# Queries one group further ahead, numerators at the front of the iteration, new orders of work

## The chip, the cores and the metric

The kernel runs on one core of a Trainium2 chip. The metric is the device time of the kernel in microseconds, as the median of several runs. The profile is of one further execution, and its times are counted from the start of its span.

## What is computed

```
xn  = (x - mean(x)) / sqrt(var(x) + 1e-5)              # x: 8 x 2048 x 256, float32
q, k, v = split(xn @ Wqkv + bqkv)                      # 256 each
qp, kp  = elu(q) + 1, elu(k) + 1
kv  = sum over s of kp[s] v[s]^T;  k_sum = sum over s of kp[s]     # per batch
attn = (qp @ kv) / (qp @ k_sum + 1e-6)
z   = layer_norm(xn + attn) * g1 + b1
h   = silu(z @ Wg + bg) * (z @ Wu + bu)                # 682 hidden columns
s   = layer_norm(z + h @ Wd + bd) * g2 + b2
g   = silu(xn @ ternary(weight)^T * scale)
out = x + s * g
```

## The kernel before

The 16384 rows are 32 groups of 512, four groups a batch; a group is four tiles of 128 rows. Float32 products are made as three products of rounded parts: every left and right operand has a high part (`_high`, written by ScalarE as fp32r) and a low part (`_low`, the rest, subtracted by VectorE). K and XK (the keys and the sum of k x^T over a batch) run five groups ahead of the feed-forward part, since kv of a batch must be known before its first numerator.

One iteration `i` works on several groups at once: the keys on group a = i + 5, its x on a + 1, the attention on q = i + 1, the feed-forward part on f = i, and the last layer norm on i - 1. The fill (i = -1) does what must be there before, iteration 31 is the end and 32 the drain. What each engine does in an iteration, and in which order, is written out by hand: a list of steps for TensorE (`TENSOR_JOBS`), ScalarE, VectorE and GpSimd, one set for the steady iterations, one for the fill, one for the end. Each engine takes its list in order and waits by semaphores; `run_steps` skips a step whose group does not exist or that the fill has done. SyncE issues all DMAs from a loop of its own.

TensorE's jobs of an iteration: K (2 jobs, 12 products of 256 columns each), Q (2 x 6 of 512), KV (2, every fourth iteration), B (2 x 8 of 256, the gate g), N (4 x 6 of 258, the numerator and denominator of a tile of 128 rows), G and U (5 each, 6 of 512), GU (one more, the last 42 hidden columns), D (five of 12 products of 256 and D 5 with 4; D 4 and D 5 come in the next iteration), XK (4 x 6 of 256). All but D and XK write to a ring of five banks: a job waits until what the fifth job before it wrote has been read. A bank of Q is freed by `q_elu`, of K by `k_add`, of N by `attn` (semaphore r), of G by `silu_gate`, of U by `h_low`, of B by `silu_tern`, of GU by `h_rows`.

The steps that the prediction names: `q_exp` (ScalarE: relu and exp of a half of q), `q_elu` (VectorE: the max with it), `q_high`, `q_low` (the parts); `k_add`, `k_exp`, `k_max`, `k_high`, `k_low` the same for the keys, `sum_k` (GpSimd) adds up kp; `x_res` (ScalarE) writes the normed x to rz, `attn` (VectorE) adds numerator times reciprocal to it and takes its statistics, `q_aggregate`, `q_rstd`, `attn_norm`, `z_rows` norm it, `z_turn` transposes it by blocks, SyncE sends it to DRAM in four pieces and reads it back, `zT_high` and `zT_low` make its parts, on which G 0 waits; `silu_gate`, `h_rows`, `h_high`, `h_low` make the hidden rows, `tail_again` (GpSimd) copies the last 32 of them twice for D 5; `ffn_rows`, `last_stats`, `last_rows`, `last_gain`, `last_offset`, `last_gate`, `last_add` finish the group before; `a_stats`, `a_norm`, `x_turn`, `x_high`, `x_low`, `xn_high`, `xn_low` prepare the next x. q, its exp and its parts have one buffer each (`qp`, `qp_h`, `qp_l`): `q_exp` of a group waits for the `q_low` of the one before, and `q_high` waits for all its N jobs. ScalarE needs another table for exp than for silu.

## Time and profile before

| | |
|---|---|
| median of three runs | 1260.41 us (1255.08 to 1262.71) |
| the profiled execution | 1252.69 us, of it the span 1251.0 us |
| TensorE busy | 1212.3 us (97%), 7499 products |
| VectorE, ScalarE, GpSimd busy | 1067.6 (85%), 957.5 (77%), 795.8 us (64%) |
| ScalarE table loads | 118, 1283 ns each |
| DMA | 116.64 MB, 93 GB/s |
| clock granted to TensorE | 0.993 of full speed |

Products overlap in the profile (each is shown some 0.17 us longer than it holds up the next), so their starts tell more than their lengths. Instructions that follow each other without a wait overlap by up to 0.1 us on the other engines too. The line of every ScalarE instruction is that of its helper (L680), and of every product L1201. A bracket behind a row gives the idle time before it and what ended it.

### The profile page before, as it was taken

Reading aid. Unit: us, or ns where it says so; the run is one execution under the profiler, and the core shown is the slowest. Engines: PE = TensorE matmul, PEld = TensorE weight load, DVE = VectorE, ACT = ScalarE, POOL = GpSimd, SP = SyncE. Lnnn points to the kernel's source line nnn. Section 1 sums busy time; section 2 is a strip of 40 time slices with the busy share of each in tenths; the row PEclk is TensorE's granted clock in tenths of the full one; section 3 lists DMA queues with packets and bytes.
Section 4 is the critical chain, followed back from the end, with each engine's and each line's share of the span. In section 5 each row is a group of like instructions: output and inputs, shape, how many; then the busy total and the mean of one; then the engine's idle time right before and its main releaser. Section 6 shows DMA issues by size and latency. Waiting matters only on the chain.

```text
span 1251.0 us, 23909 instructions
## 1 busy us (share of the span) xinstructions
PE 1212.3 (97%) x7499; PEld 1078.8 (86%) x7499; DVE 1067.6 (85%) x2473; ACT 957.5 (77%) x1540; POOL 795.8 (64%) x994
## 2 busy tenths in 40 slices
...
GB/s 193 66 71 85 82 88 75 112 119 119 99 71 85 102 119 119 100 75 81 101 118 118 117 71 93 76 119 119 118 86 81 83 107 102 68 68 68 68 52 34
DMA packets 138594, 116.64 MB, mean 93 GB/s; under 512 B 12387, under 2 KB 122853, under 8 KB 138470
## 3 DMA queue, kind: packets, MB, share of 16 engines
...
q8 instruction: 61, 1.00, 0.3%
...
## 4 chain that ended last, share of the span: by engine, by line
DVE 43%; PE 31%; ACT 11%; issue 11%; DMA 2%; SPq 1%; POOL 1%; DVEq 0%; ACTq 0%; POOLq 0%
PE bank L1201 21%; DVE st L887 7%; PE d_bank L1201 6%; DVE bank L1038 5%; DVE rz L997 4%; PE xk_bank L1201 3%; DVE ht L1052 3%; ACT rz L680 3%; DVE xa L928 3%; DVE xn L917 2%; DVE h_l L1048 2%; ACT hs L680 2%; ACT h_h L680 2%; DVE qp L979 2%; DVE kp L957 2%
## 5 line engine op out<-in xcount | busy, mean ns | idle before, releaser
L1201 PE MATMUL bank<-zT_h,wgu_h 128*128 128x512 f32 x704 | 279.2, 397 | 5.8 <-DVE zT_l L1028 5.8
L1201 PE MATMUL bank<-zT_l,wgu_h 128*128 128x512 f32 x704 | 279.4, 397 | 0.0
L1201 PE MATMUL bank<-zT_h,wgu_l 128*128 128x512 f32 x704 | 279.2, 397 | 0.0
L596 POOL TENSOR_TENSOR ksum<-ksum,kp 128x256 f32<-128x256 f32 x120 | 90.5, 754 | 183.8 <-DVE kp L964 182.6
L680 ACT ACTIVATE h_h<-bank 128x512 fp32r<-128x512 f32 x160 | 95.1, 595 | 133.5 <-DVE bank L1038 133.5
L1201 PE MATMUL d_bank<-wd_l,h_h 128*128 128x256 f32 x640 | 180.6, 282 | 0.0
L1201 PE MATMUL d_bank<-wd_h,h_h 128*128 128x256 f32 x640 | 180.3, 282 | 0.1
L1201 PE MATMUL d_bank<-wd_h,h_l 128*128 128x256 f32 x640 | 180.4, 282 | 0.0
L1201 PEld LDWEIGHTS bank<-zT_l,wgu_h 128*128 128x128 f32 x704 | 132.7, 189 | 31.8
L1201 PEld LDWEIGHTS bank<-zT_h,wgu_h 128*128 128x128 f32 x704 | 132.7, 189 | 30.4 <-issue 6.5
L1201 PEld LDWEIGHTS bank<-zT_h,wgu_l 128*128 128x128 f32 x704 | 133.2, 189 | 24.4
L680 ACT ACT_TABLE_LOAD x118 | 151.4, 1283 | 3.4 <-PEq L1396 0.8
L680 ACT ACTIVATE hs<-bank,hb 128x512 f32<-128x512 f32 x192 | 131.0, 682 | 28.4 <-PE bank L1201 27.7
L1048 DVE TENSOR_TENSOR h_l<-bank,h_h 128x512 fp32r<-128x512 f32 x160 | 109.7, 686 | 28.3 <-ACT h_h L680 24.9
L573 POOL TENSOR_TENSOR rstd<-ve,neg_half 128x4 f32<-128x4 f32 x64 | 66.4, 1038 | 104.9 <-DVE ve L898 104.9
L1038 DVE SCALAR_TENSOR_TENSOR bank<-bank,hb,hs 128x512 f32<-128x512 f32 x160 | 118.8, 742 | 9.8 <-PE bank L1201 7.7
L1201 PEld LDWEIGHTS d_bank<-wd_h,h_h 128*128 128x128 f32 x640 | 120.3, 188 | 3.6 <-DVE h_l L1048 0.3
L1201 PEld LDWEIGHTS d_bank<-wd_h,h_l 128*128 128x128 f32 x640 | 120.6, 188 | 3.0
L1201 PEld LDWEIGHTS d_bank<-wd_l,h_h 128*128 128x128 f32 x640 | 120.7, 189 | 0.0
L606 POOL TENSOR_TENSOR rz<-rz,g2b 128x256 f32<-128x256 f32 x124 | 92.3, 744 | 39.7 <-ACT rz L680 39.7
L887 DVE BATCH_NORM_STATS2 st<-rz 128x6 f32<-128x256 f32 x256 | 99.5, 420 | 4.4
L680 ACT ACTIVATE rz<-rz,nmr,rstd 128x256 f32<-128x256 f32 x128 | 71.9, 591 | 41.0 <-DVE nmr L1007 41.0
...
## 6 DMA issues: line engine op xcount, KB each, us to landing
...
```

What stands on the lines that cost most here:

```text
L573: eng.tensor_tensor(dst, ve[:, k, :], neg_half[:, 0:1].to_broadcast([P, TILES]), ALU.pow).then_inc(S[f"rs{k}"], 1)
L596: eng.tensor_tensor(ksum[:, slot, :], ksum[:, slot, :], part, ALU.add).then_inc(S["ks"], 1)
L606: eng.tensor_tensor(row_, row_, g2b[:, :], ALU.mult).then_inc(S["a"], 1)
L680: return eng.activation(out_, in_, func, **kw).then_inc(S[name], 1)
L887: eng.bn_stats(st[:, k, t, :], rows).then_inc(S[f"bn{k}"], 1)
L917: eng.tensor_scalar(normed(g)[:, t, :], xa[:, g % 2, t, :], mv[:, 0, t, 0:1], rstd0[:, g % LN0, t:t + 1], ALU.subtract, ALU.mult).then_inc ...
L928: eng.transpose(whole.rearrange("p (j t n) -> p t j n", t=TILES, n=BLOCK), xn[:, :, :].rearrange("p t (j n) -> p t j n", n=BLOCK)).then_in ...
L997: eng.scalar_tensor_tensor(out=rz[:, g % RZ, t, :], in0=num[:, 0:D], scalar=den[:, n % 2, 1:2], in1=rz[:, g % RZ, t, :], op0=ALU.mult, op1 ...
L1038: eng.scalar_tensor_tensor(out=hidden(g, c)[0:rows, :], in0=up, scalar=hb[0:rows, HC + c:HC + c + 1], in1=hs[0:rows, n % 2, :], op0=ALU.ad ...
L1048: eng.tensor_tensor(h_l[:, slot, :], hidden(g, c)[:, :], h_h[:, slot, :].bitcast(f32), ALU.subtract).then_inc(S["hl"], 1)
L1052: eng.scalar_tensor_tensor(out=part, in0=part.bitcast(f32), scalar=less_h[UT:UT + TH, 0:1], in1=hidden(g, c)[0:TH, :], op0=ALU.mult, op1=A ...
L1201: ins = eng.matmul(dst, left, right, start=first and n == 0, stop=last and n == len(pairs) - 1, **kw)
```

## The change

Q, `q_exp`, `q_elu`, `q_high` and `q_low` work on group q + 1 = i + 2 instead of q. The fill makes them for group 1 too. In the steady list of TensorE the N jobs now stand ahead of G 0, behind K 1; the Q jobs stand between U 2 and B 1. The other lists are ordered anew: on VectorE `attn` comes ahead of `h_rows 0`, `k_low` ahead of `z_turn`, `q_elu` and `q_low` in the second half; on ScalarE `zT_high` comes first, `x_res 0` and `x_res 1` ahead of `silu_gate 0` and `x_res 2`, `x_res 3` behind it, `q_exp` and `q_high` in the second half; on GpSimd `tail_again 0` and `1` follow each other and `sum_k 3` and `z_g1 3` come last. In the fill one of the three warm jobs comes earlier, `setup_gu_high_0` and `_1` come later on ScalarE, and `setup_gu_low_1` comes just ahead of `kv_bias` on VectorE. The lists of the end change a little. SyncE's program is unchanged. The diff without the lists of the end and of the fill on three engines:

```diff
--- before.py
+++ after.py
@@ -86,74 +86,75 @@
 
 LATE_D = 4
 TENSOR_JOBS = steps("""
-    Q 0, K 0, D 4, Q 1, KV 0, KV 1, D 5, K 1, G 0, U 0, G 1, U 1, G 2, B 0, N 0, N 1, U 2, N 2, B 1,
-    N 3, G 3, D 0, D 1, U 3, G 4, XK 0, U 4, XK 1, XK 2, XK 3, GU 5, D 2, D 3, TZ 0, TZ 1""")
+    K 0, D 4, KV 0, KV 1, D 5, K 1, N 0, N 1, N 2, N 3, G 0, U 0, G 1, U 1, G 2, B 0, U 2, Q 0, Q 1,
+    B 1, G 3, D 0, D 1, U 3, G 4, XK 0, U 4, XK 1, XK 2, XK 3, GU 5, D 2, D 3, TZ 0, TZ 1""")
 SCALAR_STEPS = steps("""
-    xk_copy 0, q_exp 0, zT_high 0, zT_high 1, q_high 0, q_exp 1, kv_high 0, k_exp 0, kv_high 1, x_res 0,
-    silu_gate 0, q_high 1, x_res 1, silu_gate 1, last_rows 0, h_high 0, h_high 1, x_res 2, last_rows 1,
-    silu_gate 2, last_rows 2, x_res 3, silu_tern 0, h_high 2, silu_tern 1, silu_gate 3, k_exp 1,
-    k_high 0, z_rows 0, last_rows 3, z_rows 1, k_high 1, z_rows 2, z_rows 3, silu_gate 4, h_high 3,
-    xn_high 0, h_high 4, silu_gate 5, x_high 0, x_high 1, h_high 5, xn_high 1""")
+    zT_high 0, zT_high 1, xk_copy 0, x_res 0, kv_high 0, kv_high 1, k_exp 0, x_res 1, silu_gate 0,
+    last_rows 0, x_res 2, last_rows 1, x_res 3, last_rows 2, silu_gate 1, h_high 0, h_high 1,
+    silu_gate 2, silu_tern 0, k_exp 1, last_rows 3, h_high 2, q_exp 0, q_exp 1, z_rows 0, k_high 0,
+    z_rows 1, z_rows 2, z_rows 3, silu_gate 3, k_high 1, silu_tern 1, q_high 0, x_high 0, silu_gate 4,
+    q_high 1, x_high 1, h_high 3, xn_high 0, xn_high 1, silu_gate 5, h_high 4, h_high 5""")
 VECTOR_STEPS = steps("""
-    k_add 0, q_elu 0, zT_low 0, zT_low 1, q_low 0, kv_bias 0, kv_bias 1, ffn_rows 0, q_elu 1,
-    ffn_rows 1, k_max 0, kv_low 0, last_stats 0, kv_low 1, k_add 1, h_rows 0, last_shift 0, q_low 1,
-    h_rows 1, h_low 0, h_low 1, a_stats 0, attn 0, attn 1, h_rows 2, attn 2, h_low 2, attn 3, a_norm 0,
-    q_aggregate 0, x_turn 0, attn_norm 0, k_low 0, k_max 1, k_low 1, z_turn 0, h_rows 3, h_low 3,
-    h_rows 4, h_rows 5, x_low 0, x_low 1, h_low 4, h_low 5""")
+    zT_low 0, k_add 0, zT_low 1, kv_bias 0, kv_bias 1, kv_low 0, kv_low 1, ffn_rows 0, ffn_rows 1,
+    k_add 1, last_stats 0, attn 0, last_shift 0, attn 1, attn 2, attn 3, h_rows 0, h_rows 1, h_low 0,
+    a_stats 0, h_low 1, k_max 0, h_rows 2, a_norm 0, q_aggregate 0, x_turn 0, attn_norm 0, k_max 1,
+    h_low 2, q_elu 0, q_elu 1, k_low 0, z_turn 0, h_rows 3, k_low 1, q_low 0, h_rows 4, q_low 1,
+    h_low 3, x_low 0, x_low 1, h_rows 5, h_low 4, h_low 5""")
 GPSIMD_STEPS = steps("""
-    sum_k 0, xn_low 0, last_rstd 0, last_gain 0, last_offset 0, sum_k 1, xn_low 1, last_gain 1, z_g1 0,
-    last_offset 1, last_gain 2, a_rstd 0, last_gate 0, last_gate 1, last_offset 2, q_rstd 0, sum_k 2,
-    last_gain 3, last_add 0, last_offset 3, last_gate 2, last_add 1, z_g1 1, z_g1 2, sum_k 3,
-    last_gate 3, tail_again 0, last_add 2, last_add 3, z_g1 3, tail_again 1""")
+    xn_low 0, last_rstd 0, last_gain 0, last_offset 0, last_gain 1, z_g1 0, last_offset 1, last_gate 0,
+    last_gain 2, xn_low 1, last_gate 1, a_rstd 0, q_rstd 0, last_add 0, last_add 1, last_offset 2,
+    last_gain 3, sum_k 0, sum_k 1, z_g1 1, last_offset 3, last_gate 2, z_g1 2, last_add 2, last_gate 3,
+    last_add 3, sum_k 2, tail_again 0, tail_again 1, sum_k 3, z_g1 3""")
 
...
 FILL_JOBS = fill("""
-    TX 0 0, TX 0 1, warm 9 1, K 0 0, TX 1 0, K 0 1, K 1 0, TX 1 1, XK 0 0, XK 0 1, setup_bias_0 0 0,
-    XK 0 2, XK 0 3, K 1 1, setup_bias_1 0 0, TX 2 0, TX 2 1, XK 1 0, XK 1 1, setup_bias_2 0 0, K 2 0,
-    XK 1 2, XK 1 3, K 2 1, TX 3 0, TX 3 1, Q 0 0, XK 2 0, K 3 0, XK 2 1, XK 2 2, XK 2 3, Q 0 1, TX 4 0,
-    K 3 1, TX 4 1, setup_sum 0 0, XK 3 0, XK 3 1, K 4 0, setup_transposes 0 0, XK 3 2, XK 3 3, KV 0 0,
-    KV 0 1, warm 9 2, K 4 1, B 0 0, B 0 1, N 0 0, XK 4 0, N 0 1, N 0 2, N 0 3, warm 9 0, XK 4 1, XK 4 2,
-    XK 4 3, TZ 0 0, TZ 0 1""")
+    TX 0 0, warm 9 2, TX 0 1, K 0 0, K 0 1, TX 1 0, warm 9 0, TX 1 1, K 1 0, setup_bias_0 0 0, XK 0 0,
+    XK 0 1, XK 0 2, XK 0 3, K 1 1, setup_bias_1 0 0, TX 2 0, TX 2 1, XK 1 0, XK 1 1, XK 1 2, K 2 0,
+    XK 1 3, K 2 1, TX 3 0, TX 3 1, Q 0 0, K 3 0, XK 2 0, setup_sum 0 0, XK 2 1, XK 2 2, XK 2 3,
+    setup_bias_2 0 0, K 3 1, TX 4 0, setup_transposes 0 0, Q 0 1, XK 3 0, XK 3 1, K 4 0, TX 4 1, XK 3 2,
+    XK 3 3, KV 0 0, K 4 1, KV 0 1, Q 1 0, Q 1 1, N 0 0, N 0 1, N 0 2, B 0 0, N 0 3, B 0 1, warm 9 1,
+    XK 4 0, XK 4 1, XK 4 2, XK 4 3, TZ 0 0, TZ 0 1""")
...
@@ -185,7 +186,7 @@
         return FILL_JOBS
     jobs = []
     for kind, n in order_of(i, FILL_JOBS, TENSOR_JOBS, END_JOBS):
-        g = {"K": a, "XK": a, "TX": a + 1, "G": f, "U": f, "GU": f, "D": f - 1 if n >= LATE_D else f}.get(kind, q)
+        g = {"K": a, "Q": q + 1, "XK": a, "TX": a + 1, "G": f, "U": f, "GU": f, "D": f - 1 if n >= LATE_D else f}.get(kind, q)
         if kind == "TZ" and ZT0 <= g < ZT1:
             continue
         if 0 <= g < GROUPS and (kind != "KV" or q % GPB == 0) and (kind, g, n) not in FILL_JOBS:
@@ -871,8 +872,8 @@
                     "setup_gu_high_0": (a, lambda: gu_high(0)), "setup_gu_high_1": (a, lambda: gu_high(1)),
                     "setup_d_high": (a, setup_d_high), "setup_row_0": (a, lambda: row_copy(0)),
                     "setup_row_1": (a, lambda: row_copy(1)), "setup_row_2": (a, lambda: row_copy(2)),
-                    "zT_high": (f, zT_high), "xk_copy": (q, xk_copy), "q_exp": (q, q_exp), "k_exp": (a, k_exp),
-                    "q_high": (q, q_high), "k_high": (a, k_high), "kv_high": (q, kv_high),
+                    "zT_high": (f, zT_high), "xk_copy": (q, xk_copy), "q_exp": (q + 1, q_exp), "k_exp": (a, k_exp),
+                    "q_high": (q + 1, q_high), "k_high": (a, k_high), "kv_high": (q, kv_high),
                     "silu_gate": (f, silu_gate), "x_res": (q, x_res), "h_high": (f, h_high),
                     "silu_tern": (q, silu_tern), "xT_high": (a + 1, xT_high), "x_high": (a + 1, x_high), "z_rows": (q, z_rows),
                     "xn_high": (a + 1, xn_high), "last_rows": (last, last_rows)})
@@ -1184,8 +1185,8 @@
                     "setup_d_bias": (a, setup_d_bias), "setup_q_low": (a, lambda: setup_qk_low(0)), "setup_bq": (a, setup_bq),
                     "setup_gu_low_0": (a, lambda: setup_gu_low(0)), "setup_gu_low_1": (a, lambda: setup_gu_low(1)),
                     "setup_ternary": (a, setup_ternary), "setup_ternary_parts": (a, setup_ternary_parts),
-                    "zT_low": (f, zT_low), "a_stats": (a + 1, a_stats), "q_elu": (q, q_elu), "k_add": (a, k_add),
-                    "q_low": (q, q_low), "k_max": (a, k_max), "k_low": (a, k_low), "kv_bias": (q, kv_bias),
+                    "zT_low": (f, zT_low), "a_stats": (a + 1, a_stats), "q_elu": (q + 1, q_elu), "k_add": (a, k_add),
+                    "q_low": (q + 1, q_low), "k_max": (a, k_max), "k_low": (a, k_low), "kv_bias": (q, kv_bias),
                     "kv_low": (q, kv_low), "ffn_rows": (last, ffn_rows),
                     "h_rows": (f, h_rows), "attn": (q, attn), "h_low": (f, h_low), "a_norm": (a + 1, a_norm), "x_turn": (a + 1, x_turn), "x_low": (a + 1, x_low),
                     "q_aggregate": (q, lambda g, _: aggregate(1, g)), "last_stats": (last, last_stats),
```

## Rows read from the trace of the kernel before

**Rows 1.** Windows of TensorE: stretch, its length, busy time (x products), clock granted, DMA share, GB/s.

```profile
60.00:86.00 26.00, 20.87 (x134) 0.93 0.35 99
86.00:1100.00 1014.00, 1011.55 (x6342) 1.00 0.33 96
1100.00:1225.00 125.00, 117.67 (x680) 0.99 0.22 64
```

**Rows 2.** Timeline of VectorE: start, length, operation; `h_low 5` of three iterations in a row.

```profile
636.39 2.35 DVE L1052 SCALAR_TENSOR_TENSOR ht<-ht,less_h,hs 62x512 fp32r<-62x512 f32 x1
...
674.82 2.36 DVE L1052 SCALAR_TENSOR_TENSOR ht<-ht,less_h,hs 62x512 fp32r<-62x512 f32 x1
...
711.60 2.36 DVE L1052 SCALAR_TENSOR_TENSOR ht<-ht,less_h,hs 62x512 fp32r<-62x512 f32 x1
```

**Rows 3.** Chain of waits, 624 to 642 us: start, length, engine and line.

```profile
626.02 0.99 PE xk_bank L1201 x6
627.00 1.40 PE bank L1201 x6
628.40 2.13 PE xk_bank L1201 x18
...
631.93 2.87 PE d_bank L1201 x24
```

**Rows 4.** Timeline of VectorE, 682 to 704 us: stats, next add, attn, both k_low.

```profile
682.74 1.40 DVE L887 BATCH_NORM_STATS2 st<-rz 128x6 f32<-128x256 f32 x4
...
684.88 0.68 DVE L957 TENSOR_TENSOR kp<-bank,bk1b 128x512 f32<-128x512 f32 x1
...
691.14 0.14 DVE L991 TENSOR_SCALAR den<-bank 128x1 f32<-128x1 f32 x1
...
692.38 0.14 DVE L991 TENSOR_SCALAR den<-bank 128x1 f32<-128x1 f32 x1
...
700.50 0.68 DVE L973 TENSOR_TENSOR kp_l<-kp,kp_h 128x512 fp32r<-128x512 f32 x1
...
702.75 1.08 DVE L973 TENSOR_TENSOR kp_l<-kp,kp_h 128x512 fp32r<-128x512 f32 x1 [0.97 <-ACT kp_h L680]
```

**Rows 5.** The tile xk_bank: what its engine sat idle for, us and times.

```profile
  DVE kp_l L973: 14.0, 28
```

**Rows 6.** Timeline of TensorE, the waits for z; in brackets the idle time before.

```profile
84.60 0.38 PE L1201 MATMUL bank<-wqk_h,xT_h 128*128 128x256 f32 x1 [1.26 <-DVE zT_l L1028]
...
1184.81 0.47 PE L1201 MATMUL bank<-zT_h,wgu_h 128*128 128x512 f32 x1 [1.51 <-DVE zT_l L1028]
...
1214.29 0.71 PE L1201 MATMUL d_bank<-wd_h,ht 128*128 128x256 f32 x4 [1.41 <-POOL ht L657]
1216.26 0.47 PE L1201 MATMUL bank<-zT_h,wgu_h 128*128 128x512 f32 x1 [1.25 <-DVE zT_l L1028]
```

**Rows 7.** Timeline of ScalarE: two table loads with their neighbours; rows of one iteration.

```profile
0.80 1.28 ACT L680 ACT_TABLE_LOAD   x1 [0.80 <-PEq L1396]
6.20 0.63 ACT L680 ACTIVATE wqk_h<-qp 128x512 fp32r<-128x512 f32 x1 [4.11 <-DMA qp<-in_L_attn_Wqkv_dram]
...
67.57 1.28 ACT L680 ACT_TABLE_LOAD   x1 [0.53 <-POOL wd_l L663]
...
614.41 0.60 ACT L680 ACTIVATE rz<-rz,norm 128x256 f32<-128x256 f32 x1
614.91 0.60 ACT L680 ACTIVATE rz<-xq,nmr,rstd 128x256 f32<-128x256 f32 x1
```

**Rows 8.** Timelines of VectorE and ScalarE: the last z_turn and the zT_high it feeds.

```profile
1204.50 1.25 DVE L1017 STREAM_TRANSPOSE xa<-rz 128x1024 f32<-128x1024 f32 x1 [2.64 <-ACT rz L680]
...
1213.61 1.15 ACT L680 ACTIVATE zT_h<-xa 128x512 fp32r<-128x512 f32 x2 [2.55 <-DMA xa<-z_turned]
```

**Rows 9.** Timeline of GpSimd around 636 us: last_add 2 and 3, z_g1 3.

```profile
636.08 1.42 POOL L625 TENSOR_TENSOR rz<-rz,xq 128x256 f32<-128x256 f32 x2
637.47 0.72 POOL L646 TENSOR_TENSOR rz<-rz,g1b 128x256 f32<-128x256 f32 x1
```

More of the change, by code:

```diff
@@ L112 @@
     zT_high 0, zT_high 1, silu_gate 0, h_high 0, silu_gate 1, h_high 1, silu_gate 2, last_rows 0,
-    last_rows 1, last_rows 2, silu_gate 3, h_high 2, silu_gate 4, h_high 3, last_rows 3, h_high 4,
+    last_rows 1, h_high 2, silu_gate 3, last_rows 2, last_rows 3, h_high 3, silu_gate 4, h_high 4,
     silu_gate 5, h_high 5""")
 END_VECTOR = steps("""
-    zT_low 0, zT_low 1, h_rows 0, ffn_rows 0, h_low 0, ffn_rows 1, h_rows 1, last_stats 0, h_low 1,
-    last_shift 0, h_rows 2, h_low 2, h_rows 3, h_low 3, h_rows 4, h_low 4, h_rows 5, h_low 5""")
+    zT_low 0, zT_low 1, h_rows 0, ffn_rows 0, ffn_rows 1, h_low 0, h_rows 1, last_stats 0, h_low 1,
+    last_shift 0, h_rows 2, h_low 2, h_rows 3, h_rows 4, h_low 3, h_low 4, h_rows 5, h_low 5""")
 END_GPSIMD = steps("""
-    z_g1 0, end_terms 0, z_g1 1, last_rstd 0, last_gain 0, last_offset 0, last_gate 0, last_gain 1,
-    last_offset 1, last_gain 2, z_g1 2, last_offset 2, z_g1 3, last_gain 3, last_gate 1, last_add 0,
-    last_gate 2, tail_again 0, tail_again 1, last_add 1, last_offset 3, last_add 2, last_gate 3,
+    end_terms 0, z_g1 0, last_rstd 0, last_gain 0, last_gain 1, last_offset 0, last_gain 2, z_g1 1,
+    last_gate 0, last_offset 1, last_gate 1, last_gain 3, last_offset 2, last_add 0, last_offset 3,
+    last_gate 2, z_g1 2, tail_again 0, tail_again 1, z_g1 3, last_add 1, last_add 2, last_gate 3,
     last_add 3""")
```

44 lines of the change are left out of this document (23 added, 21 removed).

## The prediction

> **What bounds the kernel now.** I read the windows of the span first, then the timelines of one steady iteration on each engine, then the chain of waits, and last the two ends of the run. The windows [rows 1] show TensorE busy for 1011.55 of the 1014 us from 86 to 1100 us. A steady iteration lasts 36.78 us without the two KV jobs (711.60 - 674.82) and 38.43 us with them [rows 2]. The chain gives the price of TensorE's jobs [rows 3]: six 512-wide products 1.40 us (0.233 each), eighteen 256-wide ones 2.13 us (0.118), twenty-four 2.87 us (0.120). An iteration has 78 wide products (eleven gate/up jobs, two Q jobs) and 152 narrow ones (K 24, B 16, N 24, D 64, XK 24): 78 x 0.233 + 152 x 0.1195 = 36.3 us. So the middle can give back less than 0.5 us an iteration. Where it is lost is one place: XK 0 takes 0.99 us for six narrow products that are worth 0.71 [rows 3], because `k_low 0` comes behind `x_turn` and `attn_norm` on VectorE and starts at 700.50 only [rows 4]; in all TensorE's two queues stood 14.0 us before XK jobs for it [rows 5]. The rest of the idle time is at the ends: 60 to 86 us (20.87 busy of 26) and 1100 to 1225 (117.67 of 125) [rows 1]. There TensorE waits for the transposed z: 1.26 us at 84.60, 1.51 at 1184.81 (one of three iterations alike), and at 1214 to 1216 D 5 and G 0 wait for 1.41 and 1.25 us [rows 6]; 3 x 1.51 + 1.41 + 1.25 = 7.2 is all the idle time of the window from 1100 on (7.3).
>
> **The change part by part.** No product, no exponential and no transfer is added. Q, `q_exp`, `q_elu`, `q_high` and `q_low` of a group run one iteration earlier; the first iteration's share (two Q jobs, 2 x 1.40 = 2.8 us of TensorE) moves into the fill and is missing at the end. SyncE's program is the same text, so its DMAs shift only with their semaphores. What changes the time is therefore who waits. I walk one steady iteration without KV, t = 0 at K 0, with TensorE's prices above and VectorE's from its timeline [rows 4].
>
> TensorE, if nothing waits: K 0 0, D 4 1.43, D 5 2.86, K 1 3.34, N 0 to N 3 4.77 to 7.69, G 0 to 9.09, U 0 to 10.49, G 1 to 11.89, U 1, G 2, B 0 to 15.64, U 2 to 17.04, Q 0 to 18.44, Q 1 to 19.84, XK 0 at 27.85, end 36.4. Five banks go round, so a job needs what the fifth before it left: U 0 needs `attn 0`, G 1 `attn 1`, U 1 `attn 2`, G 2 `attn 3`, U 2 `h_low 0`, Q 1 `h_low 1`.
>
> VectorE: `k_add 1` can start at 4.97 and ends at 5.6. `last_stats` costs 2.14 (684.88 - 682.74) and each `attn` 1.24 (692.38 - 691.14) [rows 4]: `attn 0` starts at 7.75, its row is free at 8.6 (U 0 wants it at 9.09). `attn 2` needs `x_res 2`, which stands behind `silu_gate 0` and `last_rows 0` on ScalarE. G 0 is ready at 9.3; from there silu 0.6, `last_rows` 0.50 (614.91 - 614.41, start to start) and `x_res` 0.60 [rows 7] give 11.0; the row is free at 11.5, U 1 wants it at 11.89. `attn 3` is free at 12.7 (wanted 13.29). Then `h_rows 0, 1` and `h_low 0` end at 15.1 (wanted 15.64), `a_stats` (as `last_stats`, 2.3) and `h_low 1` at 18.0 (wanted 18.44). The margins are 0.3 to 0.5 us and VectorE stands only where it waits for `x_res 2` and `h_high 0`. `k_low 0` ends at 25.5, 2.3 us ahead of XK 0 at 27.85: the old stall goes. D 5 now stands 5.7 us behind the end of GU 5 instead of 8.5, but its chain (silu 0.8, `h_rows 5` 0.7, `tail_again` twice, `h_low 5`) ends 3.9 to 4.2 us behind it. z is sent at about 25.5; from the transpose's start to landing the last group took 1213.61 - 1204.50 = 9.1 us [rows 8], so it is there 8 us before G 0 of the next iteration needs it.
>
> Terms: (a) the XK stall. At 0.28 an iteration (0.99 - 0.71) over some 19 waits it is 5.3 us; by the 14.0 us of [rows 5] it is more, though part of that stands under running products. I take -8. (b) KV iterations. D 5 comes 2.2 us later, `kv_low` stands ahead of `ffn_rows`, and `attn 0` frees its bank 0.2 to 0.3 us late; seven times, +2. (c) Collisions of VectorE with GpSimd. `k_low 1` at 702.75 took 1.08 us where the one at 700.50 took 0.68 [rows 4], both with two SBUF operands; the new order puts `zT_low 0, 1` (also two) beside `tail_again 1`, `sum_k 3`, `z_g1 3` and `xn_low 0`. If each waits for one GpSimd instruction, 0.4 us, VectorE's own slack of 0.2 us before `k_add 1` and 0.35 at U 1 leave 0.1 to 0.2 an iteration: between 0 and the 0.65 below I take 0.13 x 27 = +3. (d) The end. In the three iterations without K and XK, z is sent so much earlier that G 0 no longer waits: -1.5 each; but with no K jobs ahead U 0 comes before `attn 0` is through and waits 0.5: -3. In the last iteration no Q comes before the z rows, so the 1.41 and 1.25 us shrink to near nothing: -3, 2.7 rounded up, since the granted clock of 0.99 in that window [rows 1] shows a short stretch below 2.4 GHz. (e) The fill. Up to the TZ jobs TensorE gets 2.8 us of Q and loses one warm job (0.7); between TZ and G 0 it has K 0, K 1 and N 0 to N 3 (5.8 us) instead of K and Q (5.7). VectorE has two `q_elu` more before `attn_norm`, which comes some 0.9 us later, but ScalarE no longer keeps `zT_high` behind `q_exp`, and G 0 starts a good microsecond earlier with 2.9 us of N jobs already done. Of the 5.1 us idle in the window from 60 to 86 [rows 1] I take -3.6, with 2 to either side. The early weight copies (`gu_high` behind `k_exp 1`) save a wait of VectorE, but `setup_bias_0` now stands ahead of all XK jobs and waits for the same transfer: 0.
>
> Sum: -8 + 2 + 3 - 3 - 3 - 3.6 = -12.6, rounded to -13. It is made against the profiled execution (span 1251.0, its own time 1252.69), which lies 7.7 us below the median of 1260.41; for the median I take the same 13: 1247.4.
>
> A rule of the Trainium skill speaks against term (c). "SBUF — State Buffer", section "SBUF: two separate sides", says that a VectorE instruction with two SBUF inputs and a GpSimd instruction that reads SBUF share one port pair, held whole by whoever comes first. The 1.08 us above agrees with it. By it alone, with a free turn between two GpSimd instructions, the sum stays about as it is.
>
> **The rivals.**
> *Collisions cost a full turn.* `h_low 5` took 2.35 us at 636.39 [rows 2] while GpSimd ran three additions and products back to back until 638.19 [rows 9]: it got no turn in between. If `zT_low 1` fares so and waits until `xn_low 0` ends at 4.25, `k_add 1` ends 1.1 us late, and U 0 and U 1 wait 0.65: 27 x 0.65 = 17.6 instead of 3, so +2 us in all: 1262.
> *Starved twice, slower than before.* If `zT_low 0` waits that long too, `k_add 1` ends at 7.9 instead of 5.6 and U 0 waits 1.8 us in each iteration: 27 x 1.8 = 48.6 instead of 3, sum +33: 1293. It decides against the change from 0.6 us an iteration on, where it eats up the other terms. For it speaks the 2.35; against it that `k_low`, of zT_low's form, got in after one turn.
> *Table load behind G 0.* `silu_gate 0` needs the silu table after `k_exp 0`. A load costs 1.28 us and stood ahead of the wait of its activation at 0.80, but behind a second wait at 67.57 [rows 7]. `silu_gate 0` has G 0 first and an older semaphore second. If the load waited for G 0, `x_res 2` would come at 12.3 and U 1 wait 0.95: 27 x 0.95 = 25.7, sum +10: 1270.
> *The ends give nothing.* If z is held by another step, terms (d) and (e) are 0: -3, 1257.4.
>
> **How the numbers follow.** Forecast (-20 to -8): 0.54. One full turn: 0.13. Starved twice: 0.12. Table load: 0.08. Ends give nothing: 0.13. About 1% (12.6 us) is what a measurement of this kernel can tell from no change, and the forecast's centre lies on it; since (c) and (e) may well be smaller than I took them and (a) larger (the 14.0 us), I put 0.40 of its 0.54 beyond. Within 1% lie 0.14 of the forecast, one turn, 0.10 of the case "ends" and half the table case: 0.41. Slower: starved, the other half of the table case and 0.03 of "ends": 0.19. The range reaches from 1236 (the forecast without (b) and (c), and 6 us of scatter between runs) to 1271, just past the table case; outside lie the starved case and 0.08 of tails.
>
> **What would show it.** (a) right: no XK product waits for `kp_l`. (c) right: `zT_low` near 0.7 to 1.1 us, few waits of U 0 and U 1 for `attn`; wrong: waits of TensorE on `rz` of `attn` in every iteration and a period above 36.8. (d): no wait of 1.5 us for `zT_l` after 1100. (e): G 0 of the first group at 84 to 86 us, N jobs before it. Table: a load that ends before G 0 does. The prediction is wrong if the period does not fall below 36.8 us.

## The result

| | before | after |
|---|---|---|
| median of 4 runs each | 1259.41 us (1255.08 to 1262.71) | 1238.27 us (1236.89 to 1239.85) |
| the profiled execution | 1252.69 us, span 1251.0 | 1236.89 us, span 1235.0 |
| clock granted to TensorE | 0.993 | 0.998 |
| TensorE, VectorE, ScalarE, GpSimd busy | 1212.3, 1067.6, 957.5, 795.8 us | 1205.2, 1081.2, 949.5, 860.0 us |

The ratio of the runs is 0.9835, 95% interval [0.98, 0.9869]: 1.65% faster, by 21 us in the median and by 16 in the profiled execution. The windows of TensorE in the profile after, with the columns of [rows 1]:

```profile
60.00:86.00 26.00, 23.08 (x157) 1.00 0.35 93
86.00:1100.00 1014.00, 1010.52 (x6352) 1.00 0.33 96
1100.00:1225.00 125.00, 123.27 (x723) 1.00 0.22 64
```

Both ends are fuller (20.87 and 117.67 us busy before). The windows hold different work, so a clean ledger needs a marker with the same work ahead of it in both kernels. D 5 is one: when D 5 of an iteration starts, both lists have done the same jobs, Q and N too. Timeline of TensorE before, its first D 5, the one of the 26th iteration and the last:

```profile
120.58 0.64 PE L1201 MATMUL d_bank<-wd_h,ht 128*128 128x256 f32 x4
...
1049.92 0.64 PE L1201 MATMUL d_bank<-wd_h,ht 128*128 128x256 f32 x4
...
1241.32 0.71 PE L1201 MATMUL d_bank<-wd_h,ht 128*128 128x256 f32 x4 [0.73 <-POOL ht L657]
```

The same three after (lines have moved by one):

```profile
113.66 0.65 PE L1202 MATMUL d_bank<-wd_h,ht 128*128 128x256 f32 x4
...
1039.67 0.65 PE L1202 MATMUL d_bank<-wd_h,ht 128*128 128x256 f32 x4
...
1225.36 0.71 PE L1202 MATMUL d_bank<-wd_h,ht 128*128 128x256 f32 x4 [0.43 <-POOL ht L658]
```

Up to the first D 5 the new kernel gains 6.9 us (forecast 3.6), over the 25 periods behind it 3.3 (forecast 8 - 2 - 3 = 3), from there to the end 5.7 (forecast 6): 16.0 in all against 12.6. Some 5 us of these 16.0 are stretches at 1.2 GHz in the profiled execution of before, as the last part shows under (d) and (e). Without KV, a period from D 5 to D 5 is 36.64 us on average before and 36.42 after (19 of them); the six with KV are 38.82 to 38.90 before and 38.54 to 39.34 after. TensorE's waits for `kp_l` [rows 5] are gone from the middle: the three that are left lie in the fill, at 72 to 74 us. The row of the tile xk_bank that answers [rows 5]:

```profile
  DVE kp_l L974: 3.5, 3
```

Timeline of VectorE after, a steady iteration, `h_low 5` to `zT_low 1` around K 0 at 629.57:

```profile
628.80 0.75 DVE L1053 SCALAR_TENSOR_TENSOR ht<-ht,less_h,hs 62x512 fp32r<-62x512 f32 x1
629.58 0.99 DVE L1029 TENSOR_TENSOR zT_l<-xa,zT_h 128x512 fp32r<-128x512 f32 x1
630.49 0.68 DVE L958 TENSOR_TENSOR kp<-bank,bk1b 128x512 f32<-128x512 f32 x1
631.09 0.68 DVE L1029 TENSOR_TENSOR zT_l<-xa,zT_h 128x512 fp32r<-128x512 f32 x1
```

Timeline of GpSimd after, beside it: `tail_again 1`, `sum_k 3`, `z_g1 3`:

```profile
628.94 1.09 POOL L658 CAST ht<-hs 32x512 fp32r<-32x512 f32 x1 [0.22 <-POOL ht L658]
630.11 1.05 POOL L597 TENSOR_TENSOR ksum<-ksum,kp 128x256 f32<-128x256 f32 x1
631.12 1.24 POOL L647 TENSOR_TENSOR rz<-rz,g1b 128x256 f32<-128x256 f32 x1
```

`h_low 5`, 2.35 us in the old order [rows 2], takes 0.75, `zT_low` 0.99 and 0.68; it is GpSimd whose `z_g1` takes 1.24 instead of the 0.72 of [rows 9]. Timeline of ScalarE after, the table load of silu and `silu_gate 0`:

```profile
598.22 1.28 ACT L681 ACT_TABLE_LOAD   x1
600.72 0.69 ACT L681 ACTIVATE hs<-bank,hb 128x512 f32<-128x512 f32 x1 [1.22 <-PE bank L1202]
```

The table load is over at 599.50, while G 0 still runs: the rival "table load behind G 0" didn't come.

### The profile page after: what moved, and what is told of

Same layout as the page of the kernel before. It is cut to its first block, busy times and chain, and to the rows that moved or that the text cites. A ratio compares the mean times of both kernels' runs of the same rounds, so it can differ in the third digit from the quotient of the medians.

```text
span 1235.0 us, 23906 instructions
## 1 busy us (share of the span) xinstructions
PE 1205.2 (98%) x7499; PEld 1078.8 (87%) x7499; DVE 1081.2 (88%) x2473; ACT 949.5 (77%) x1538; POOL 860.0 (70%) x994
## 4 chain that ended last, share of the span: by engine, by line
PE 79%; DVE 6%; DMA 5%; ACT 3%; issue 3%; SPq 2%; POOL 1%; DVEq 0%; ACTq 0%; POOLq 0%
PE bank L1202 57%; PE d_bank L1202 15%; PE xk_bank L1202 7%; ACT rz L681 1%; DMA xa<-z_turned 1%; DMA xa<-turned 1%; DVE st L888 1%; DMA turned<-xa 1%; DMA z_turned<-xa 1%; DVE xT_l L935 1%; ACT qp L681 1%; DVE bank L1039 1%; ACT hs L681 1%; DVE h_l L1049 1%; DVE xn L918 0%
## 5 line engine op out<-in xcount | busy, mean ns | idle before, releaser
L597 POOL TENSOR_TENSOR ksum<-ksum,kp 128x256 f32<-128x256 f32 x120 | 117.6, 980 | 18.3 <-DVE kp L965 10.9
L647 POOL TENSOR_TENSOR rz<-rz,g1b 128x256 f32<-128x256 f32 x128 | 118.8, 929 | 0.4
L626 POOL TENSOR_TENSOR rz<-rz,xq 128x256 f32<-128x256 f32 x124 | 111.2, 908 | 2.4
```

Source lines behind the costliest of these rows:

```text
L597: eng.tensor_tensor(ksum[:, slot, :], ksum[:, slot, :], part, ALU.add).then_inc(S["ks"], 1)
L626: eng.tensor_tensor(row_, row_, xq[:, g % 3, t, :], ALU.add).then_inc(S["o"], 1)
L647: eng.tensor_tensor(row_, row_, g1b[:, :], ALU.mult).then_inc(S["zg"], 1)
```

## The experiments

Twelve kernels, each beside runs of the kernel before on the same chip; all ratios are to that kernel, whose medians there were 1257.88 to 1258.28 us. After was not run again beside them, so "over after" compares medians of different chips (4 runs of after), and a few us of it are only as good as the profile that goes with them. "Period" is from D 5 to D 5.

### The fill's orders alone

Before, with the four lists of the fill of after, less the steps of group 1.

```diff
-    TX 0 0, TX 0 1, warm 9 1, K 0 0, TX 1 0, K 0 1, K 1 0, TX 1 1, XK 0 0, XK 0 1, setup_bias_0 0 0,
+    TX 0 0, warm 9 2, TX 0 1, K 0 0, K 0 1, TX 1 0, warm 9 0, TX 1 1, K 1 0, setup_bias_0 0 0, XK 0 0,
...
```

> The kernel before with the four fill lists of the changed kernel, less the Q steps of group 1; steady and end lists as before. Theory (the fill gained 7.7 us of the 16, of it about 2.8 before the first KV job through the order of the setup work): the first KV job starts near 57.0 us instead of 59.0, and the kernel is 2 to 4 us faster than before (ratio 0.997 to 0.9985), since what was won by Q behind KV and N ahead of G 0 needs the new steady lists. Rival (the fill's gain is all from Q and N in the gap before G 0): KV job at 59, ratio 1.000. Rival (whole fill gain from these orders): 7 us, ratio 0.9945.

Measured 1257.71 us (10 runs), ratio 0.9996 [0.997, 1.0022]. The first D 5 came at 119.64, 0.9 us early; the first KV product at 58.38, not near 57.0 as I expected. The granted clock between 20 and 30 us was 0.83, as before. The new orders of the fill by themselves are worth next to nothing. Three of its 25 periods were 2.5 us too long; the next kernels show what such a period is.

### k_low 0 first

```diff
-    q_aggregate 0, x_turn 0, attn_norm 0, k_low 0, k_max 1, k_low 1, z_turn 0, h_rows 3, h_low 3,
+    q_aggregate 0, k_low 0, x_turn 0, attn_norm 0, k_max 1, k_low 1, z_turn 0, h_rows 3, h_low 3,
```

> The kernel before with one step moved: k_low 0 ahead of x_turn and attn_norm in the steady list of VectorE. Theory: the wait of XK 0 for kp_l (14.0 us in 28 idle spells) goes, the period without KV falls from 36.79 to 36.45, in all 6 to 9 us faster (ratio 0.993 to 0.995). Rival (TensorE loses the same time at another wait, as the changed kernel did, whose middle gained 3.4 us only): the wait goes but the time falls by 0 to 3 us, ratio 0.998 to 1.000.

Measured 1281.19 us, ratio 1.020 [1.0163, 1.0236]: my theory fell. Periods are mostly 37.3 to 37.5 (39.6 with KV), two are 4.5 us longer, and TensorE now waits for the other half. Timeline of VectorE of this kernel:

```profile
720.12 0.69 DVE L973 TENSOR_TENSOR kp_l<-kp,kp_h 128x512 fp32r<-128x512 f32 x1
720.73 1.24 DVE L928 STREAM_TRANSPOSE xa<-xn 128x1024 f32<-128x1024 f32 x1
721.89 0.12 DVE L1007 SCALAR_TENSOR_TENSOR nmr<-mv,rstd 128x4 f32<-128x4 f32 x1
724.19 1.17 DVE L973 TENSOR_TENSOR kp_l<-kp,kp_h 128x512 fp32r<-128x512 f32 x1 [1.57 <-ACT kp_h L680]
```

`attn_norm` (L1007) slips behind `k_low 0`, ScalarE's first z row, which needs it, slips too (722.05, after 1.96 us idle), and `k_high 1`, behind that row, reaches `k_low 1` only at 724.19. Here a VectorE step that waits for ScalarE was put ahead of the step ScalarE waits for.

### XK 0 one job later

```diff
-    N 3, G 3, D 0, D 1, U 3, G 4, XK 0, U 4, XK 1, XK 2, XK 3, GU 5, D 2, D 3, TZ 0, TZ 1""")
+    N 3, G 3, D 0, D 1, U 3, G 4, U 4, XK 0, XK 1, XK 2, XK 3, GU 5, D 2, D 3, TZ 0, TZ 1""")
```

> The kernel before with one job moved: XK 0 stands behind U 4 instead of ahead of it, so XK 0 asks for the low parts of the keys one wide job (1.40 us) later. Only TensorE's list changes. Counted from the starts of the products, the kernel before loses about 7 us between 90 and 1085 us in front of XK jobs (18 places), and the period without KV is 36.79 us against 36.3 of bare products. Theory (term a is real and lies in this one wait): the waits of TensorE for kp_l between 86 and 1100 us vanish, the period falls by about 0.3 us, and the run gets 6 to 9 us shorter (ratio about 0.994). Rival (the loss is only moved: U 4, GU 5 or D 2 then stand for their hidden rows, or the next iteration's first jobs do): waits for kp_l vanish too, but waits for the silu or h_high take their place, and the run is within 2 us of before.

Measured 1261.38 us (10 runs), ratio 1.0023 [0.999, 1.0056]: no gain. Most of its periods are those of before: with XK 0 served, XK 2 waits for `k_low 1` (its weight load 0.34 us in an ordinary iteration, XK 0's some 0.6 before). Both halves of `k_low` were late, and moving one, or the job that asks for one, frees nothing; no run moved both halves and nothing else. Four of its periods, though, were 3 to 4.5 us too long, and the profile of before has none of that kind. One of them, timeline of TensorE in this kernel, K 0:

```profile
339.88 0.36 PE L1201 MATMUL bank<-wqk_h,xT_h 128*128 128x256 f32 x1 [2.82 <-DVE xT_l L934]
```

Timeline of VectorE in this kernel, the two steps of `x_low`, which take 1.28 us in an ordinary iteration:

```profile
336.04 3.70 DVE L934 TENSOR_TENSOR xT_l<-xa,xT_h 128x512 fp32r<-128x512 f32 x2 [0.60 <-ACT xT_h L680]
```

Timeline of GpSimd beside it, `last_add 2`, `last_add 3` and `z_g1 3`:

```profile
336.07 1.41 POOL L625 TENSOR_TENSOR rz<-rz,xq 128x256 f32<-128x256 f32 x2
337.45 0.71 POOL L646 TENSOR_TENSOR rz<-rz,g1b 128x256 f32<-128x256 f32 x1
```

In an ordinary iteration of the old order `x_low` ends just ahead of this run of three and `h_low 5` pays for it (2.35 us, harmless). Here ScalarE had to wait 0.71 us for the transposed x, so `x_low` started beside the run and ended 1.6 us behind it, and K 0 stood for 2.8 us.

### sum_k 3 late, in the old order

```diff
-    sum_k 0, xn_low 0, ... z_g1 1, z_g1 2, sum_k 3, last_gate 3, tail_again 0, ... z_g1 3, tail_again 1
+    sum_k 0, xn_low 0, ... z_g1 1, z_g1 2, last_gate 3, tail_again 0, ... z_g1 3, tail_again 1, sum_k 3
```

> The kernel before with sum_k 3 (GpSimd's last addition to the sum of the keys) moved behind tail_again 1, where the changed kernel has it about. Theory (the KV iterations of the changed kernel became dearer because KV 0 finds the key sum unfinished, not because of D 5 or attn): every KV iteration gets a wait of TensorE for the key sum, 0.5 to 0.8 us, seven times, +3 to +5 us, and the iterations without KV stay as they are, unless the addition collides with VectorE's zT_low. Rival (forecast's reason for term b: D 5 later, kv_low ahead of ffn_rows): no effect on KV iterations, time within 1 us of before.

Measured 1259.85 us (10 runs), ratio 1.0011 [0.9973, 1.0048]. The KV periods that weren't of the long kind stayed at 38.5 to 38.8, and TensorE never waited for the key sum: in the old list Q 0 and Q 1 stand ahead of KV 0, and those 2.8 us cover the addition. The test missed its aim, but shows what the new list gives up. Six of its periods were of the long kind, with `x_low` at 3.5 to 3.8 us for the pair.

### sum_k 3 early, in the new order

```diff
-    last_add 3, sum_k 2, tail_again 0, tail_again 1, sum_k 3, z_g1 3""")
+    last_add 3, sum_k 2, sum_k 3, tail_again 0, tail_again 1, z_g1 3""")
```

> The changed kernel with sum_k 3 moved on GpSimd from behind tail_again 1 to right behind sum_k 2, where GpSimd stood idle 1.4 us. Theory: the wait of 0.5 to 0.8 us of the KV jobs for the key sum goes in five to seven iterations and zT_low meets one GpSimd instruction less: 3 to 5 us faster than the changed kernel, 1233 to 1235. Rival (tail_again comes later and D 5 waits instead): same or up to 5 us slower, 1238 to 1243.

Measured 1236.26 us (4 runs), ratio 0.9839 [0.9812, 0.9867]. KV periods fall from 38.5 to 39.3 to a steady 38.5; the 25 periods take 924.1 us instead of 926.0. That is -1.9, less than expected: the KV periods gave 3.0, but the other 19 took 1.1 more (one of 37.1 and one of 36.8 among them). In the median it is hardly to be told from after. In after the first KV product does wait for the key sum (0.47 us of idle time at 631.30); here none does. This is the fastest kernel of the study, by a margin that these runs don't establish.

### The silu table load behind G 0

After, with the two waits of `silu_gate 0`, and of it alone, exchanged (a branch for c = 0 does it), so that the load comes behind the wait for G 0.

```diff
-                if c < HF:
+                if c == 0:
+                    if n >= 2:
+                        eng.wait_ge(S["h"], n - 1)
+                    eng.wait_ge(S["G"], 2 * (HF * g + c) + 1)
+                    src = job_bank("G", g, c)
+                elif c < HF:
...
-                if n >= 2:
+                if n >= 2 and c:
                     eng.wait_ge(S["h"], n - 1)
```

> The changed kernel with the two waits of silu_gate 0 exchanged, so that the load of the silu table comes behind the wait for G 0. Theory: silu_gate 0 and so x_res 2 come 1.3 us later, attn 2 frees its bank 1.3 us later, U 1 waits 0.8 to 1.0 us in some 27 iterations: 22 to 27 us slower than the changed kernel, 1260 to 1265. Rival (other slack takes it up): within 3 us of the changed kernel, 1238 to 1241.

Measured 1269.69 us, ratio 1.0103 [1.0074, 1.0132], 31 us over after. Timeline of ScalarE in this kernel:

```profile
616.58 1.28 ACT L681 ACT_TABLE_LOAD   x1 [2.62 <-PE bank L1207]
617.87 0.69 ACT L681 ACTIVATE hs<-bank,hb 128x512 f32<-128x512 f32 x1
```

Its waits (who for whom, us in all, times, longest), those on the rows of `attn`:

```profile
DVE rz L1003 <- ACT rz L681: 51.0, 30, 2.1
PEld bank L1207 <- DVE rz L1003: 36.2, 31, 1.3
PE bank L1207 <- DVE rz L1003: 23.0, 29, 0.9
```

The rival's price was near (0.95 us an iteration forecast; the 25 periods grew by 30.0, 1.2 each), only its condition wasn't met. The new order lives on ScalarE's margin there.

### GpSimd's additions beside zT_low

```diff
-    last_gain 3, sum_k 0, sum_k 1, z_g1 1, last_offset 3, last_gate 2, z_g1 2, last_add 2, last_gate 3,
-    last_add 3, sum_k 2, tail_again 0, tail_again 1, sum_k 3, z_g1 3""")
+    last_gain 3, sum_k 0, sum_k 1, z_g1 1, last_offset 3, last_gate 2, z_g1 2, last_gate 3,
+    sum_k 2, sum_k 3, tail_again 0, tail_again 1, last_add 2, last_add 3, z_g1 3""")
```

> The changed kernel with GpSimd's last additions moved beside VectorE's zT_low: sum_k 3 goes ahead of tail_again 0, and last_add 2, last_add 3 and z_g1 3 follow each other behind tail_again 1, ready to run without a wait, as around 636 us in the kernel before, where h_low 5 (0.75 us bare) took 2.35. It doubles the suspected cost of the forecast's term c. Rival of the forecast (VectorE gets no turn between back-to-back GpSimd instructions): zT_low 0 or 1 takes 1.4 to 2.4 us, k_add 1 ends up to 1.1 us late or more, U 0 and U 1 wait for attn, and the run gets 15 us or more longer than the changed kernel's 1238. Theory (VectorE gets in after the instruction that is running, and GpSimd is the one stretched): zT_low stays under 1.3 us each, no new wait of TensorE above 0.2 us, within 3 us of the changed kernel.

Measured 1390.97 us, ratio 1.1068 [1.1024, 1.1111], some 150 us over my theory. The time is on the rival's side, but not by its mechanism: `zT_low` was hardly touched (0.99 and 0.67 us at 656.76 and 658.27; at most 1.23 in any iteration), and `last_add 3`, beside its second half, was the one stretched, to 1.24 us. What broke was SyncE's queue. Its timeline in this kernel:

```profile
651.24 0.38 SPq L449 DMA_DIRECT2D xa<-z_turned  x1
659.58 0.39 SPq L522 DMA_DIRECT2D out_dram<-rz  x1
660.02 0.51 SPq L422 DMA_DIRECT2D xq<-in_L_attn_x_dram  x1
```

The store of the last group waits for `last_add 3`, and the load of x for `x_res` stands behind the store. Timeline of ScalarE in this kernel, `x_res 0`:

```profile
665.77 0.60 ACT L681 ACTIVATE rz<-xq,nmr,rstd 128x256 f32<-128x256 f32 x1 [8.69 <-DMA xq<-in_L_attn_x_dram]
```

Timeline of TensorE in this kernel, U 0 waiting for a bank of `attn` (G 1 and U 1 then wait 1.38 and 1.32 us):

```profile
667.01 0.50 PE L1202 MATMUL bank<-zT_h,wgu_h 128*128 128x512 f32 x1 [2.19 <-DVE rz L998]
```

Periods become 40.5 to 44.2 us. In after the same load goes out at 626.03, 3.5 us ahead of K 0, and ScalarE already waits for it in 29 iterations, 38.9 us in all, under cover.

### x sent out later

```diff
-    a_stats 0, h_low 1, k_max 0, h_rows 2, a_norm 0, q_aggregate 0, x_turn 0, attn_norm 0, k_max 1,
-    h_low 2, q_elu 0, q_elu 1, k_low 0, z_turn 0, h_rows 3, k_low 1, q_low 0, h_rows 4, q_low 1,
+    a_stats 0, h_low 1, k_max 0, h_rows 2, a_norm 0, q_aggregate 0, attn_norm 0, k_max 1,
+    h_low 2, q_elu 0, q_elu 1, x_turn 0, k_low 0, z_turn 0, h_rows 3, k_low 1, q_low 0, h_rows 4, q_low 1,
```

> The changed kernel with one step moved on VectorE: x_turn 0 stands behind q_elu 1 instead of ahead of attn_norm 0, so the next x goes out to DRAM for its transpose some 3 us later. In the kernel before, its four pieces are issued 10.8 us ahead of K 0 in every iteration, in the changed kernel 13.9; where K 0 waited for the low part of x (xT_l), in three kernels built on the order of before, the lead had grown to 13.6, that is by the wait. Theory (the changed order also made the kernel robust against a slow transfer, and that part of the gain shows in the median but not in the undisturbed profile): the lead falls back to 10.5 to 11, single iterations of 39 to 42 us come back, the runs spread over more than 5 us, and the median rises by 3 to 12 us over the changed kernel's 1238. Rival (the scatter is bound to another part of the order of before, such as ScalarE's x_high behind silu_gate 5): spread stays at 2 to 3 us and the median within 2 us of 1238.

Measured 1370.0 us, ratio 1.0889 [1.085, 1.0928]. Neither theory: every period is 41.1 to 43.6 us while K runs. Timeline of ScalarE in this kernel, `x_high 0` and `silu_gate 4`:

```profile
657.84 0.63 ACT L681 ACTIVATE xT_h<-xa 128x512 fp32r<-128x512 f32 x1 [5.52 <-DMA xa<-turned]
658.38 0.67 ACT L681 ACTIVATE hs<-bank,hb 128x512 f32<-128x512 f32 x1
```

Timeline of TensorE in this kernel, the first product of a D job:

```profile
661.35 0.58 PE L1202 MATMUL d_bank<-wd_h,h_h 128*128 128x256 f32 x1 [3.17 <-DVE h_l L1049]
```

The new list has `x_high 0` ahead of `silu_gate 4`; it stands there until the transposed x is back, and the hidden rows queue behind it. In after the same wait is there too, 23.1 us in 26 iterations, under cover.

### K 0 later in the old order

```diff
-    Q 0, K 0, D 4, Q 1, KV 0, KV 1, D 5, K 1, ...
+    Q 0, D 4, K 0, Q 1, KV 0, KV 1, D 5, K 1, ...
-    k_add 0, q_elu 0, zT_low 0, ...
+    q_elu 0, k_add 0, zT_low 0, ...
```

> The kernel before with D 4 ahead of K 0 on TensorE (and q_elu 0 ahead of k_add 0 on VectorE, so that it isn't kept back), so K 0 asks for the transposed x 1.43 us later; nothing else changes. Theory (the scatter of the kernel before, 1252 to 1272 us, comes from iterations in which the transposed x returns late): the lead of the transfer over K 0 grows from 10.8 to 12.2 us, waits for xT_l become rare, the runs spread less and the median falls from 1258 to 1252 to 1255 us. Rival (no such cause): median and spread as before, within 2 us.

Measured 1270.22 us (1259.12 to 1293.08), ratio 1.0076 [1.004, 1.0111]: slower and wider. K 0 no longer waited, but D 4, now ahead of it, did, for `h_low 4`, which stands behind `x_low` on VectorE: some 0.25 us in an ordinary iteration, 3.33 at 453.98, where `x_low` took 3.84 us beside the same run of GpSimd. So asking for the transfer later is not the cure; whichever product hangs on VectorE's queue behind the collision pays. The waits for `h_low 4` make the periods 0.3 us longer, 7 us over the 25, which is the greater part of the 12 us by which the median rose; the rest is not settled: the profiled execution, with one such iteration, took 1260.15, among the shortest of the twelve.

### The old fill under the new lists, twice

After, with the fill's lists of before and the steps of group 1 put in.

```diff
...
-    KV 0 1, warm 9 2, K 4 1, B 0 0, B 0 1, N 0 0, XK 4 0, N 0 1, N 0 2, N 0 3, warm 9 0, XK 4 1, XK 4 2,
+    KV 0 1, warm 9 2, K 4 1, Q 1 0, Q 1 1, B 0 0, B 0 1, N 0 0, XK 4 0, N 0 1, N 0 2, N 0 3, ...
```

> The changed kernel with the fill in the order of the kernel before; only what it must have for group 1 (two Q jobs, q_exp, q_elu, q_high, q_low) is put in. Theory (the gain of the fill comes from the steady lists that take over behind it: four N jobs ahead of G 0 and ScalarE's zT_high at the front, not from the orders within the fill): KV 0 0 starts as late as before at the same granted clock, G 0 of the first group starts within 2 us of the changed kernel's 82.12, and the run is 1 to 3 us longer than the changed kernel, about 1239 us. Rival (the new orders of the fill carry it): 5 to 8 us longer, 1243 to 1246.

Measured 1249.09 us, ratio 0.9921 [0.9899, 0.9944], 10.8 over after: the rival was nearer. KV 0 0 starts at 57.60 (after 56.94), but G 0 of the first group at 90.61 instead of 82.12; on the way K 0 waits, timeline of TensorE in this kernel:

```profile
83.17 0.55 PE L1203 MATMUL bank<-wqk_h,xT_h 128*128 128x256 f32 x1 [2.52 <-DVE xT_l L936]
```

The second run has `x_high` of group 5 ahead of `x_res 3` and the z rows on ScalarE.

```diff
-    x_res 0 2, k_exp 4 1, q_exp 1 1, silu_tern 0 0, silu_tern 0 1, k_high 4 1, q_high 1 0, x_res 0 3,
+    x_res 0 2, k_exp 4 1, q_exp 1 1, silu_tern 0 0, silu_tern 0 1, k_high 4 1, q_high 1 0, x_high 5 0,
+    x_high 5 1, x_res 0 3, z_rows 0 0, z_rows 0 1, z_rows 0 2, z_rows 0 3, q_high 1 1, xn_high 5 0,
```

> The changed kernel with the fill in the order of the kernel before and group 1 put in, as in the earlier run that took 1249 us, but with x_high of group 5 ahead of x_res 3 and the z rows on ScalarE, where the changed kernel has it, and the weight tail's bias step moved on VectorE. In the earlier run K 0 of the first iteration waited 2.52 us for xT_l, and the granted clock was 0.66 between 80 and 90 us. Theory (the fill's new orders are worth something only because group 1's steps now lie in it and would otherwise push x_high and the z rows back): that wait goes, G 0 of the first group starts at 84 to 87 us, and the run takes 1240 to 1244 us. Rival (it is the early part of the fill, up to KV 0): still 1247 to 1250.

Measured 1244.95 us, ratio 0.9893 [0.9847, 0.9939], 4.1 less than the first, 6.7 over after, where I expected 2 to 6. The wait of K 0 is gone, but the first XK product that needs `kp_l` now waits 3.60 us at 77.96 where it waited 1.51, so G 0 starts only 1.6 us sooner (89.02), and the clock granted is 0.85 and 0.81 between 70 and 80 and between 80 and 90 us. With the first kernel of this section: the fill's orders are worth nothing without group 1 and 7 to 11 us with it. They let the moved work in without a stall; how much of the 7 to 11 us is due to where I put group 1's steps in the old lists, and how much to the clock, isn't settled.

### The old end under the new lists

```diff
-    end_terms 0, z_g1 0, last_rstd 0, ...
+    z_g1 0, end_terms 0, z_g1 1, last_rstd 0, ...
...
```

> The changed kernel with the four lists of iteration 31 (the end) of the kernel before. Theory (the forecast's term d comes from iterations 28 to 30, where z is sent earlier and nothing of Q stands ahead of the z rows): within 1 us of the changed kernel's 1238. Rival (the end lists carry part of it): 2 to 4 us longer.

Measured 1242.09 us, ratio 0.9872 [0.9833, 0.9911], 3.8 over after: the rival. Up to iteration 30 the profile is that of after; then, timeline of VectorE with the old end:

```profile
1200.42 3.92 DVE L1029 TENSOR_TENSOR zT_l<-xa,zT_h 128x512 fp32r<-128x512 f32 x2 [1.37 <-ACT zT_h L681]
```

Timeline of GpSimd with the old end, `z_g1` and the start of `end_terms`:

```profile
1199.61 1.43 POOL L647 TENSOR_TENSOR rz<-rz,g1b 128x256 f32<-128x256 f32 x2
1201.27 2.53 POOL L633 TENSOR_TENSOR rz<-sg,b2b 128x1024 f32<-128x1024 f32 x1 [0.22 <-DMA out_dram<-rz]
```

Timeline of VectorE in after:

```profile
1200.34 1.29 DVE L1029 TENSOR_TENSOR zT_l<-xa,zT_h 128x512 fp32r<-128x512 f32 x2 [1.46 <-ACT zT_h L681]
```

With `z_g1 0` in front, `zT_low` starts while GpSimd is busy, and its second half waits for the whole of `end_terms` (2.53 us). G 0 waits 3.65 us instead of 1.12. That is 2.5 of the 4.0 us by which the last period is longer (29.35 against 25.34); right behind this wait lies a stretch of 3.4 us at 1.2 GHz, from 1204.7 on, which after has not. In after `zT_low` is first and `end_terms` is the one stretched (2.72).

## Why the prediction was right, and where it wasn't

The verdict, faster by more than 1%, was in the forecast, and so was the sum: 1238.27 lies in the range, 9 us below the forecast of 1247.4, and the terms taken together missed the profiled execution by 3.4 us (16.0 against 12.6). That nearness hides two things: the sum had next to nothing for the clock, and without the clock's share in (d) and (e) the terms measure about 11.

- *What bounds the kernel.* Held. The middle gave 3.3 us over 25 iterations, the ends 12.6, of which about 5 are the clock.
- *(a) XK.* The waits for `kp_l` went as said. The 19 periods without KV fell from 36.64 to 36.42 us on average, 4.1 in all; the six with KV, of 38.88, are 38.5 once the key sum is out of their way (`sum_k 3` early), 2.3 more. That makes 6.4, where I had 8 less 3 for (a) and (c) together. The cause I named, `k_low 0` behind `x_turn`, was a part of it: two experiments show TensorE waiting for `k_low 1` as soon as `k_low 0` is served (in the first of them the edit had also made it later). That only both together help is the reading that fits; no run tried it alone.
- *(b) KV.* The six KV periods grew by 0.7 us in all though the XK wait left them too. With `sum_k 3` early they take 3.0 us less than in after, so (b) is 3, not 2; and the cause was another. The waits that the profile shows are for `sum_k 3`, not for D 5 or `attn`: with Q out of the way, KV 0 asks 2.8 us sooner, and with the addition put forward the KV periods are 38.5.
- *(c) Collisions.* Sized wrongly: I charged the new order 3 us for them, and the trace shows none. `zT_low` takes 0.99 and 0.68 us (a half never more than 1.22 between 115 and 1130 us), with GpSimd stretched instead, and TensorE doesn't wait for the rows of `attn` in a steady iteration. The old order had the longer ones: `h_low 5` at 2.35 us in nearly every iteration, which cost TensorE nothing, and `x_low` at 3.5 to 4.2 us now and then, which did. I had read the 2.35 [rows 2, 9] and used it only against the change.
- *(d) The end.* 5.7 against 6, but 1.6 of it is the clock, so the mechanism gave about 4. In the three iterations without K, G 0 no longer waits 1.5 us and U 0 waits 0.2, not 0.5. In the last one D 5 no longer waits 1.41, but G 0 still waits 1.12 us; I had its wait at near nothing. The last period, from D 5 to D 5, has one stretch at 1.2 GHz in before, right behind two waits of TensorE (from 1217.1 on). Window of TensorE of this period, columns as in [rows 1], in before:

```profile
1214.29:1241.32 27.03, 25.04 (x131) 0.94 0.03 9
```

  and in K 0 later, which has the same lists of the end:

```profile
1223.54:1248.76 25.22, 23.49 (x131) 1.00 0.03 10
```

  Three of the kernels with the old lists of the end have no such stretch and take 25.2 to 25.4 us, like after (25.34). Four of the seven profiles with these lists have it and none of the seven with the new ones. The lists of the end I had not priced at all; the old ones would cost 3.8 us.
- *(e) The fill.* 6.9 up to the first D 5, where I had 3.6, and the difference is the clock, which the sum left out. Two stretches of 3.4 us at 1.2 GHz lie in the fill of before, from 25.9 and from 77.1 us on. Windows of TensorE, columns as in [rows 1], in before:

```profile
20.00:30.00 10.00, 7.39 (x25) 0.83 0.54 158
70.00:80.00 10.00, 7.39 (x40) 0.85 0.17 59
```

  in the kernel with `sum_k 3` late, which has the fill of before:

```profile
20.00:30.00 10.00, 8.36 (x35) 1.00 0.53 159
70.00:80.00 10.00, 7.11 (x45) 1.00 0.15 54
```

  and its first D 5, 3.4 us sooner than in before:

```profile
117.16 0.64 PE L1201 MATMUL d_bank<-wd_h,ht 128*128 128x256 f32 x4
```

  Against it after (113.66, no such stretch) gains 3.5 us. Two more kernels with the old fill and no stretch start G 0 of the first group 0.8 and 1.0 us later than this one, so 3.5 to 4.5 is the fill at full clock. G 0 came at 82.12 where I had 84 to 86 us. A stretch comes and goes with the execution. Window of TensorE in after:

```profile
20.00:30.00 10.00, 7.89 (x35) 1.00 0.54 161
```

  and in the kernel with `sum_k 3` early, which has the fill of after, and whose first D 5 comes at 115.64, 2.0 us later:

```profile
20.00:30.00 10.00, 7.54 (x25) 0.83 0.60 167
```

  That the setup's order is worth 0 held alone, but not with group 1 in it.
- *The median.* 21 us against 16 in the profile. The step that failed is "for the median I take the same". The profiled execution of before had not one long iteration; its relatives in the old order had one to six each, 2.3 to 5 us too long, and the runs of the kernel before spread over 1252 to 1268 us, with one at 1272. The six kernels in the new order whose transfers were left in place had none over 1.5 us too long, and the runs of each (4 only) lie within 4 us: GpSimd's run of three is broken up there (`last_gate 3`, `sum_k 2` and `tail_again` stand in it), and `x_low` takes 1.7 to 2.4 us for the pair in nearly every iteration, with cover. The kernel with the fill's orders alone has before's steady and end lists; its profiled execution took 1257.05, close to its median of 1257.71, and held three long iterations, its 25 periods taking 936.2 us where those of before took 929.3. So a few long iterations a run can well make up the missing 5 us. This is inferred: no run of before with such an iteration was profiled. The clock is no part of these 5 us: the profiled execution of before was granted 0.993 of full speed, like the median of its runs (0.993 to 0.994, all within 0.989 to 0.996). But after's runs have 0.996 to 0.998, so the clock's share of the 16 us is in the medians too. By my estimate from 0.993 and 0.998 over 1250 us it is 6 us at most. Whether the new order's fewer waits brought it, no run shows.
- *The rivals.* "One full turn" and "starved twice" didn't come: `zT_low` takes at most 1.22 us a half and `h_low 5` 0.75 in every steady iteration. Their mechanism is real and was in the kernel before. "Table load": refuted, its price confirmed to about a quarter. Its sum was wrong: the 25.7 us came in place of the 3 for collisions, which the table has nothing to do with; added to the other terms they give +13 and 1273.5, outside the range. "The ends give nothing": refuted, the ends gave most, with the clock's share or without.
